# Moving the output projection, two score visits and the masks inside a hand-scheduled attention block

## The chip, the cores and the metric

The kernel runs on one core of one Trainium2 chip. The metric is the device time of one execution in microseconds (us). "Before" is the kernel as it stood, with a median of 557.84 us over three runs.

TensorE (PE in the profile) does matmuls, VectorE (DVE), ScalarE (ACT) and GpSimd (POOL) do the rest, and SyncE (SP) issues the transfers. Each runs its own instruction stream and waits on semaphores.

## The reference, cut to what matters

The input is `x` of 2 sequences of 2048 tokens with 128 features. The reference is one attention layer and one feed-forward layer, each with a normalised residual:

```python
qkv = x @ qkv_w + qkv_b                      # 16 heads of 8
local = softmax(q k^T * scale, dist in (0, 128]) v     # a window of 128 tokens
lattn = softmax(rq rk^T * lscale, over up to 64 pooled latents)
remote = (lattn @ rv) @ rout_w + rout_b
gate = sigmoid(local @ gl_w + remote_h @ gr_w)
mixed = gate * local + (1.0 - gate) * remote_h
y = mixed @ out_w + out_b                    # the output projection
x = x + layernorm(y)
x = x + layernorm(ffn(layernorm(x)))         # 4 experts, argmax router
```

Softmax is computed from a row maximum, so every score is needed twice: once with queries on the partitions (for the maximum) and once with keys on the partitions (for the product with the values).

## The kernel before

**Stages.** The function before `attend` loads, normalises and multiplies by the weights (roughly the first 70 us). `attend` computes both attentions and adds the layer's output to `X`. `ffn` follows; its engines start only when `attend`'s last instructions are done.

**Blocks and steps.** `attend` takes the 4096 tokens as 32 blocks of 128 (`NB` = 32, 16 for each sequence). It runs steps s = -2 to 34, and each engine has one function `emit(s)` with the work of step s in a fixed order. A step works on several blocks at once: the maxima of block s+2, the scores of block s, the latents' product and the values' last part of block s-1, the mixing and projection of block s-2, the output's normalisation of block s-3.

**Visits.** On PE and ACT a step has eight visits g = 0 to 7, each for a pair of heads in both halves. At a visit PE issues:
- `score(s + 2, g, a)` into `psS[g % 2]` (lines 925 to 928), which waits until DVE has taken the maxima of two visits earlier;
- `score_t(s, g, a)` into `psST[g % 2]` (line 961), which waits for the exponentials of two visits earlier;
- then what else belongs to the visit.

**The rest of a step on PE, before the change.** Visit 0: transposes of the latents' probabilities `lprob` of block s-1 (line 1014). Visit 1: `values(s - 1, 3)`. Visit 2: the latents' product into `psC` for block s-1 (line 1025) and the latents' scores (line 1031). Visit 3: transpose of the negated maxima (line 1038), `values(s, 0)`. Visit 4: transposes of `mixed` (line 1049) and of the products with the values (line 1055). Visit 5: `values(s, 1)`. Visit 6: the output projection of block s-2 (line 1064) into `psC`. Visit 7: `values(s, 2)`. These other matmuls are fp32, the scores are bf16.

**Masks.** Scores outside the window must not count. For the visits in `SELECTED` GpSimd sets the exponentials to zero afterwards (`select`, lines 1216 and 1219: two instructions, each 128 x 256). For the other visits PE adds the mask to the bank before the scores (`mask_t`, line 949). The first block of a sequence has all its masks by PE. `values(n, G)` waits for the exponentials of visits 2G and 2G+1 and for the last of the selects that belong to them.

**GpSimd's order in a step before.** The three small operations on the maxima of block s+1 (lines 1230 to 1236); three small operations for the normalisation of block s-3 (`yve`, `yrstd`, `ybias`, lines 1244 to 1249); select of visit 0; `gdiff` and `mixed` of block s-2; selects of visits 2, 3 and 4; `diff` of block s-1 (line 1276); `lprob` of block s (line 1283); select of visit 6; the addition into `X` of block s-3 (line 1290). `select(n, g)` waits for the exponential of visit g.

**ScalarE's order.** At each visit the exponential of that visit (line 1304), and behind it: visit 0 the copy of `lprobT`; visit 2 the copy of the products; visit 3 `mT`; visit 4 `mixedT` and two latent heads' exponentials (line 1343); visit 5 two more; visit 6 `yn` (line 1355); visit 7 `ez`, which waits for `diff`.

**VectorE's order.** Two maxima a visit (line 1084), with others between them: visit 0 `bn_aggr` of block s-3, `ez1`, `gate`; visit 3 the remote part (line 1153) and `lmin`; visit 4 `rden`; visit 5 the local part (line 1180); visit 6 `lrs`; visit 7 `y` (line 1195) and `bn_stats` (line 1199) of block s-2. In the last steps DVE also does, at visit 1, the next stage's `norm.apply` (steps 33 and 34) and `norm.statistics` (steps 32 and 33), and GpSimd does `norm.deviations` near the start of steps 33 and 34.

**Latents.** A block in the first half of its sequence uses 32 latents, one in the second half 64. So `lprob` has 128 or 256 columns, and visits 0 and 2 have one or two rounds.

Of the kernel before, what the change touches and what calls it, by code (L numbers as in the profile page):

```python
# [22 lines left out]
ALU = mybir.AluOpType  # L23
# [3 lines left out]
B, S, D = 2, 2048, 128  # L27
# [27 lines left out]
VW = HZ + 1  # L55
HALF_LAT = NLAT // 2
UN = H // 2
SELECTED = (0, 2, 3, 4, 6)
PAIR_OF_ONES = 1.0 + 2.0 ** -9 - 2.0 ** -16
EPS = 1e-5  # L60
LN_EPS = 1e-12
# [682 lines left out]
def attend(nc, held, for_ffn, norm, ident, identb, filler, eps_col, mhalf, X, lat_k, lat_v, scratch, s_load, s_out):  # L744
    with ExitStack() as ctx:
# [15 lines left out]
        wout, bout, brout, minus1 = held.wout, held.bout, held.brout, held.minus1  # L761
# [25 lines left out]
        mixedT = sb("mixedT", [P, P])  # L787
        y = sb("y", [P, 2, D])
        ystats = sb("ystats", [P, 6])
        ymv = sb("ymv", [P, 2, 2])  # L790
        yve = sb("yve", [P, 1])
        yrstd = sb("yrstd", [P, 1])
        ybias = sb("ybias", [P, 1])
# [7 lines left out]
        psC = ps("psC", [P, 512])  # L801
# [25 lines left out]
        s_local = signal("s_local", "dve")  # L827
# [85 lines left out]
        def _(pe):  # L913
# [75 lines left out]
            def emit(s):  # L989
                for g in range(UN):  # L990
# [9 lines left out]
                    for a in range(2):  # L1000
                        if (s + 2).live:
                            score(s + 2, g, a)
                            if not s.live:
                                beside((psA, psC)[(g + 1) % 2], (g + 1) % 2, 2 * P)
                        if s.live:
                            if not (s + 2).live:
                                beside(psS[g % 2][:].rearrange("p a k -> p (a k)"), g % 2, 2 * P)
                            score_t(s, g, a)
                    if g == 0 and (s - 1).live:
                        n = s - 1  # L1010
                        pe.wait_ge(s_lprob.sem, s_lprob.after(n))
                        pe.wait_ge(s_mixTc.sem, s_mixTc.after(n - 2))
                        for f in range(lat_of(n) // HALF_LAT):
                            last = nc.tensor.transpose(psLP[:, f * P:(f + 1) * P],
                                                       lprob[:, f * P:(f + 1) * P], ident[:])
                        last.then_inc(s_lpT.sem, 1)
# [40 lines left out]
                        last.then_inc(s_pvT.sem, 1)  # L1057
                    if g == 5 and s.live:
                        values(s, 1)
                    if g == 6 and (s - 2).live:  # L1060
                        n = s - 2
                        pe.wait_ge(s_mixTc.sem, s_mixTc.after(n))
                        pe.wait_ge(s_local.sem, s_local.after(n + 1))
                        nc.tensor.matmul(psC[:, 0:D], mixedT[:], wout[:], start=True,
                                         stop=True).then_inc(s_proj.sem, 1)
                    if g == 7 and s.live:
                        values(s, 2)

# [4 lines left out]
        def _(dve):  # L1073
# [48 lines left out]
            def emit(s):  # L1122
                for g, a in ((g, a) for g in range(UN) for a in range(2)):
# [8 lines left out]
                    if (g, a) == (1, 0) and isinstance(s.i, int) and NB <= s.k < NB + 2:  # L1132
                        dve.wait_ge(s_x1.sem, s_x1.after(step(0, CT * (s.k - NB + 1) - 1)))
                        norm.statistics(dve, chunk(s.k - NB))
                    if (g, a) == (0, 0) and (s - 3).live:
                        n = s - 3
                        dve.wait_ge(s_ystats.sem, s_ystats.after(n, 1))
                        stand(dve, s_pass_dve)
                        nc.vector.bn_aggr(ymv[:, n.mod(2)], ystats[:]).then_inc(s_ystats.sem, 1)
# [43 lines left out]
                    if (g, a) == (6, 0) and s.live:  # L1183
# [3 lines left out]
                        if s.mod(RING) == 0:  # L1187
                            dve.wait_ge(s_lrs.sem, s_lrs.after(s))
                            nc.vector.tensor_scalar(lrs[:], lrs[:], valid[:, 1, bass.ds(s.over(RING), 1)],
                                                    None, ALU.mult).then_inc(s_lval, 1)  # L1190
                    if (g, a) == (7, 0) and (s - 2).live:
                        n = s - 2
                        dve.wait_ge(s_proj.sem, s_proj.after(n))
                        dve.wait_ge(s_yn.sem, s_yn.after(n - 2))
                        nc.vector.tensor_tensor(y[:, n.mod(2)], psC[:, 0:D], bout[:], ALU.add).then_inc(s_y.sem, 1)
                    if (g, a) == (7, 1) and (s - 2).live:
                        n = s - 2
                        dve.wait_ge(s_y.sem, s_y.after(n))
                        nc.vector.bn_stats(ystats[:], y[:, n.mod(2)]).then_inc(s_ystats.sem, 1)

# [3 lines left out]
        def _(pool):  # L1204
# [17 lines left out]
            def emit(s):  # L1222
# [14 lines left out]
                      .then_inc(s_neg.sem, 1)  # L1237
                if isinstance(s.i, int) and s.k > NB:
                    norm.deviations(pool, chunk(s.k - NB - 1))
                if (s - 3).live:  # L1240
                    n = s - 3
                    pool.wait_ge(s_ystats.sem, s_ystats.after(n))
                    pool.wait_ge(s_yn.sem, s_yn.after(n - 1))
                    nc.gpsimd.tensor_tensor(yve[:], ymv[:, n.mod(2), 1:2], eps_col[:, 0:1],
                                            ALU.add).then_inc(s_yrstd.sem, 1)
                    pool.wait_ge(s_yrstd.sem, s_yrstd.after(n, 1))
                    nc.gpsimd.tensor_tensor(yrstd[:], yve[:], mhalf[:, 0:1], ALU.pow).then_inc(s_yrstd.sem, 1)
                    pool.wait_ge(s_yrstd.sem, s_yrstd.after(n, 2))
                    nc.gpsimd.tensor_scalar(ybias[:], ymv[:, n.mod(2), 0:1], yrstd[:, 0:1], -1.0, ALU.mult,
                                            ALU.mult).then_inc(s_yrstd.sem, 1)  # L1250
                if s.live:
                    select(s, SELECTED[0])
                if (s - 2).live:
# [12 lines left out]
                                            ALU.add).then_inc(s_mix.sem, 1)  # L1266
                if s.live:
                    select(s, SELECTED[1])
                    select(s, SELECTED[2])
                    select(s, SELECTED[3])  # L1270
                if (s - 1).live:
# [560 lines left out]
```

## Time and profile before

| what | value |
|---|---|
| three runs | 556.84, 557.84, 561.45 us |
| profiled execution | 561.67 us |
| its span, first to last instruction | 560.0 us |
| busy share of the span: PE, DVE, ACT, POOL | 92%, 75%, 53%, 58% |
| mean granted TensorE clock, as a share of full speed | 0.959 |
| length of a step in mid-sequence, 64 latents | 8.62 us |
| length of a step in mid-sequence, 32 latents | 8.41 us |
| last instruction of `attend` ends at | 375.2 us |

The length of a step is the distance between the same matmul in neighbouring steps of the timeline. A row of the timeline gives start, duration, engine, line, operation, tiles and shapes; behind it in brackets stands how long the engine had been idle and what released it. A matmul's duration is modelled, its start is recorded, so distances between starts are the safe reading.

### The profile page before, as it was taken

To read this page: it belongs to the slowest core of one execution; us is meant where nothing else is said; L and a number is where in the kernel's file an instruction comes from. 1 tells how busy PE (TensorE), PEld (TensorE's weight loads), DVE (VectorE), ACT (ScalarE), POOL (GpSimd) and SP (SyncE) were. 2 spreads that over 40 slices of the span, in tenths; PEclk is the share of its full clock that TensorE was granted. 3 is DMA by queue.
4 is the path that set the end of the run, shared out by engine and by line. 5 is a ranking of instruction groups with operands and counts; after the bars stand their busy time and mean duration, and the time that the engine had idled before them with its cause. 6 is when DMAs were issued, how large, how long until landed. Compare 5 with 4: busy or idle time off the path is not lost. (4 is left out here: it accounts for less than half of the span.)

```text
span 560.0 us, 16868 instructions
## 1 busy us (share of the span) xinstructions
PE 515.8 (92%) x5405; PEld 326.1 (58%) x5408; DVE 420.8 (75%) x1952; ACT 298.4 (53%) x820; POOL 325.1 (58%) x759
## 2 busy tenths in 40 slices
PE   8999779999999999999999998869999999999991
PEld 4766424555556665555555665435677677677671
DVE  5876486989888888989898887645647767775655
ACT  2545405888888888888888888612222212211210
POOL 4454301788888888688888889960122342333341
PEclk9999855999999999999999999997999999999997
DMA  4466550434112322222322100000000000000001
GB/s 128 132 193 186 158 104 2 100 88 74 35 41 59 81 62 57 48 36 63 62 63 46 21 4 3 3 1 0 1 2 1 20 17 2 19 19 1 20 19 38
DMA packets 49059, 28.11 MB, mean 50 GB/s; under 512 B 6808, under 2 KB 48056, under 8 KB 48976
## 3 DMA queue, kind: packets, MB, share of 16 engines
q1 hardware_dynamic: 47648, 26.73, 19.7%
q8 instruction: 42, 0.69, 0.5%
q10 hardware_dynamic: 1328, 0.36, 0.3%
q14 instruction: 41, 0.34, 0.2%
HBM read 17.90 MB, written 8.91 MB: 48 GB/s over the span
## 5 line engine op out<-in xcount | busy, mean ns | idle before, releaser
L1084 DVE CUSTOM_DVE_ANT_0 added<-psS,maskq 128x256 bf16<-128x256 f32 x512 | 200.7, 414 | 35.5 <-PE psS L925 22.4
L1304 ACT ACTIVATE probs<-psST 128x512 f32<-128x512 f32 x240 | 143.4, 598 | 42.5 <-PE psST L961 40.9
L961 PE MATMUL psST<-qst,kst 50*128 50x128 bf16 x992 | 100.8, 221 | 0.0
L925 PE MATMUL psS<-kst,qst 48*128 48x256 bf16 x448 | 91.3, 286 | 3.6 <-DVE rowmax L1084 1.6
L982 PE MATMUL psPV<-probs,vst 128*10 128x128 f32 x1984 | 79.7, 276 | 12.7 <-POOL probs L1219 8.9
L1748 ACT ACTIVATE hT<-fpsH 128x512 f32<-128x512 f32 x32 | 19.2, 599 | 121.6 <-PE fpsH L1492 121.6
L1216 POOL TENSOR_SCALAR_AFFINE_SELECT probs<-probs 128x256 f32<-128x256 f32 x150 | 62.1, 414 | 4.1 <-ACT probs L1304 3.5
L925 PEld LDWEIGHTS psS<-kst,qst 48*128 48x128 bf16 x448 | 25.1, 95 | 63.2 <-issue 37.2
L1219 POOL TENSOR_SCALAR_AFFINE_SELECT probs<-probs 128x256 f32<-128x256 f32 x150 | 61.6, 411 | 0.0
L982 PEld LDWEIGHTS psPV<-probs,vst 128*10 128x10 f32 x1984 | 43.9, 91 | 28.1 <-issue 17.4
L1489 PE MATMUL fpsH<-xehi,w1hi 128*128 128x512 f32 x128 | 55.7, 435 | 0.0
L961 PEld LDWEIGHTS psST<-qst,kst 50*128 50x128 bf16 x992 | 55.6, 95 | 0.0
L1489 PE MATMUL fpsH<-xelo,w1hi 128*128 128x512 f32 x128 | 50.6, 395 | 0.0
L1489 PE MATMUL fpsH<-xehi,w1lo 128*128 128x512 f32 x128 | 50.5, 395 | 0.0
L1084 DVE DVE_READ_ACCUMULATOR2_ANT rowmax<- 128x1 f32 x512 | 42.2, 82 | 0.0
L949 PE MATMUL psST<-maskk,identb 128*128 128x512 bf16 (+1 forms) x106 | 39.8, 375 | 0.0
L1731 POOL TENSOR_TENSOR y<-y,gamma 128x512 f32<-128x512 f32 x7 | 9.0, 1293 | 51.9 <-DVE y L1676 51.9
L1343 ACT ACTIVATE lexp<-psA,lmin 128x64 f32<-128x64 f32 (+1 forms) x128 | 37.3, 304 | 0.0
L1668 DVE TENSOR_TENSOR xehi<-fpsE,xfThi 128x512 fp32r<-128x512 f32 x32 | 22.0, 688 | 19.7 <-issue 10.0
L1532 PE MATMUL fpsY<-wo,hT 128*128 128x128 f32 x256 | 30.6, 278 | 0.7 <-ACT hT L1748 0.7
L1489 PEld LDWEIGHTS fpsH<-xehi,w1hi 128*128 128x128 f32 x128 | 24.0, 188 | 11.9 <-issue 8.4
L602 POOL TENSOR_TENSOR early<-resid,early 128x512 bf16<-128x512 f32 x16 | 18.4, 1169 | 20.9 <-ACT early L650 20.9
(198 smaller groups left out, 1111.6 us busy)
## 6 DMA issues: line engine op xcount, KB each, us to landing
q_parts<-early SPq DMA_DIRECT2D x8, 384.0 KB, 2.6
k_parts<-early SPq DMA_DIRECT2D x8, 384.0 KB, 2.7
qst<-q_parts SPq DMA_DIRECT2D x32, 96.0 KB
kst<-k_parts SPq DMA_DIRECT2D x32, 96.0 KB
X<-in_L_attn_x_dram SPq DMA_DIRECT2D x8, 256.0 KB, 3.2
qst<-q_parts SPq DMA_DIRECT2D x32, 64.0 KB
kst<-k_parts SPq DMA_DIRECT2D x32, 64.0 KB
out_dram<-res SPq DMA_DIRECT2D x8, 256.0 KB, 2.3
```

The lines of the kernel that those rows point to most:

```text
L925: last = nc.tensor.matmul(bank[:, a], q, kst[rows, slot, ring(n - 1, 2)], start=True, stop=True)
L949: nc.tensor.matmul(psST[g % 2][:].rearrange("p a (s q) -> p a s q", s=2)[:, :, sides[0]:2], identb[:], maskk[:, sides[0]:2].unsqueeze(1).b ...
L961: last = nc.tensor.matmul(bank[:, a, side * P:(side + 1) * P], kst[rows, slot, ring(n - 1 + side)], qst[rows, slot, ring(n)], start=not ma ...
L982: last = nc.tensor.matmul(psPV[32 * t:32 * t + VW, G * P:(G + 1) * P], vst[:, n.k - 1 + side, SLOTS * (t // 2) + 2 * G + a, :], probs[:, u ...
L1084: taken = nc.vector.tensor_tensor_reduce(added[:, 2 * (g % 2) + a], psS[g % 2][:, a], mask, 1.0, NEG * 4, ALU.add, ALU.max, rowmax[:, n.mo ...
L1216: nc.gpsimd.affine_select(out=before, in_=before, compare_op=ALU.is_gt, fill=0.0, base=0, pattern=[[0, 2], [1 - P, P]], channel_multiplier=P)
L1219: nc.gpsimd.affine_select(out=own, in_=own, compare_op=ALU.is_gt, fill=0.0, base=0, pattern=[[0, 2], [1, P]], channel_multiplier=-1).then_ ...
L1304: nc.scalar.activation(probs[:, g ^ 1], psST[g % 2][:].rearrange("p a c -> p (a c)"), ACT.Exp, scale=SCALE).then_inc(s_exp.sem, 1)
L1343: nc.scalar.activation(per_lat(lexp, s)[:, h], per_lat(psA, s)[:, h], ACT.Exp, bias=lmin[:, s.mod(2), h:h + 1], scale=-1.0, accum_out=lsum ...
L1489: nc.tensor.matmul(psH[j % 2][:], w[:, e, tile], x[:, u, e], start=(e == 0 and k == 0), stop=False)
L1532: last = nc.tensor.matmul(psY[:, t * P:(t + 1) * P], hT[:, m.mod(2), j, t * P:(t + 1) * P], wo[:, j], start=(j == 0), stop=(j == IT - 1))
L1668: nc.vector.tensor_tensor(xehi[:, u, e], psE[e % 2][:], xfThi[:, u].bitcast(F32), ALU.mult)
```

## The change

- PE issues the output projection of block s-3 at visit 0, ahead of the `lprob` transposes, in place of block s-2 at visit 6. It gains a wait for `y` of the block before.
- DVE does `y` and `bn_stats` at visit 1 (block s-3) in place of visit 7 (block s-2), and `bn_aggr` at visit 2 in place of visit 0. In `emit` they stand behind `norm.apply` and `norm.statistics` of visit 1.
- Visits masked by GpSimd become 0, 2, 4, 6 and 7; those masked by PE become 1, 3 and 5. Visit 6 then has only its scores, and visit 7 has no mask.
- GpSimd's order becomes: maxima, select 0, `gdiff`, `mixed`, select 2, `yve`/`yrstd`/`ybias`, select 4, select 6, `diff`, `lprob`, select 7, `X`.

```diff
-SELECTED = (0, 2, 3, 4, 6)
+SELECTED = (0, 2, 4, 6, 7)
...
+                    if g == 0 and (s - 3).live:
+                        n = s - 3
+                        pe.wait_ge(s_mixTc.sem, s_mixTc.after(n))
+                        pe.wait_ge(s_local.sem, s_local.after(n + 1))
+                        pe.wait_ge(s_y.sem, s_y.after(n - 1))
+                        nc.tensor.matmul(psC[:, 0:D], mixedT[:], wout[:], start=True,
+                                         stop=True).then_inc(s_proj.sem, 1)
                     if g == 0 and (s - 1).live:
...
-                    if g == 6 and (s - 2).live:
-                        n = s - 2
-                        pe.wait_ge(s_mixTc.sem, s_mixTc.after(n))
-                        pe.wait_ge(s_local.sem, s_local.after(n + 1))
-                        nc.tensor.matmul(psC[:, 0:D], mixedT[:], wout[:], start=True,
-                                         stop=True).then_inc(s_proj.sem, 1)
...
-                    if (g, a) == (0, 0) and (s - 3).live:
+                    if (g, a) == (2, 0) and (s - 3).live:
                         n = s - 3
                         dve.wait_ge(s_ystats.sem, s_ystats.after(n, 1))
...
-                    if (g, a) == (7, 0) and (s - 2).live:
-                        n = s - 2
+                    if (g, a) == (1, 0) and (s - 3).live:
+                        n = s - 3
                         dve.wait_ge(s_proj.sem, s_proj.after(n))
...
-                    if (g, a) == (7, 1) and (s - 2).live:
-                        n = s - 2
+                    if (g, a) == (1, 1) and (s - 3).live:
+                        n = s - 3
                         dve.wait_ge(s_y.sem, s_y.after(n))
...
                 if s.live:
                     select(s, SELECTED[1])
+                if (s - 3).live:
+                    n = s - 3
+                    pool.wait_ge(s_ystats.sem, s_ystats.after(n))
+                    pool.wait_ge(s_yn.sem, s_yn.after(n - 1))
...
+                if s.live:
                     select(s, SELECTED[2])
                     select(s, SELECTED[3])
                 if (s - 1).live:
```

The added lines in GpSimd's order are those of `yve`, `yrstd` and `ybias`, which leave their place ahead of the first select. The last part of the order stays in place in the code: `diff`, `lprob`, `select(s, SELECTED[4])`, `X`.

## Rows read from the trace of the kernel before

**Rows 1.** Windows, one step with 64 and one with 32 latents; busy us, clock.

```profile
core 0: us, PE busy (x) PEld busy (x) DVE busy (x) ACT busy (x) POOL busy (x), PEclk, DMA share, GB/s
203.04:211.67 8.63, 8.43 (x147) 5.30 (x146) 7.50 (x45) 7.36 (x24) 7.54 (x21) 1.00 0.39 87
245.51:253.92 8.41, 7.91 (x130) 4.92 (x130) 7.43 (x45) 7.16 (x24) 7.33 (x21) 1.00 0.09 25
```

**Rows 2.** Timeline of PE, visits 5, 6, 7 of step 14, then 0.

```profile
209.56 0.23 PE L927 MATMUL psS<-kst,qst 48*128 48x128 bf16 x1
...
210.14 0.62 PE L982 MATMUL psPV<-probs,vst 128*10 128x128 f32 x16 [0.18 <-POOL probs L1219]
210.70 0.23 PE L927 MATMUL psS<-kst,qst 48*128 48x128 bf16 x1
...
210.88 0.22 PE L961 MATMUL psST<-qst,kst 50*128 50x128 bf16 x1
211.03 0.49 PE L1064 MATMUL psC<-wout,mixedT 128*128 128x128 f32 x2
211.36 0.38 PE L949 MATMUL psST<-maskk,identb 128*128 128x512 bf16 x1
211.67 0.23 PE L927 MATMUL psS<-kst,qst 48*128 48x128 bf16 x1
...
212.56 0.28 PE L925 MATMUL psS<-kst,qst 48*128 48x256 bf16 x1
...
212.88 0.44 PE L1014 MATMUL psB<-ident,lprob 128*128 128x128 f32 x2
```

**Rows 3.** Timeline of GpSimd over the same stretch.

```profile
210.89 0.49 POOL L1276 TENSOR_TENSOR diff<-both 128x144 f32<-128x144 f32 x1 [0.17 <-DVE both L1180]
211.89 0.61 POOL L1283 TENSOR_TENSOR lprob<-lexp,lrs 128x256 f32<-128x256 f32 x1 [0.51 <-DVE lrs L1186]
212.45 0.41 POOL L1216 TENSOR_SCALAR_AFFINE_SELECT probs<-probs 128x256 f32<-128x256 f32 x1
212.81 0.41 POOL L1219 TENSOR_SCALAR_AFFINE_SELECT probs<-probs 128x256 f32<-128x256 f32 x1
```

**Rows 4.** Timeline of ScalarE, the exponentials of visits 5 and 6.

```profile
210.04 0.60 ACT L1304 ACTIVATE probs<-psST 128x512 f32<-128x512 f32 x1
...
211.17 0.60 ACT L1304 ACTIVATE probs<-psST 128x512 f32<-128x512 f32 x1
```

**Rows 5.** Timeline of VectorE: the maxima of visit 5, later y.

```profile
210.15 0.42 DVE L1084 CUSTOM_DVE_ANT_0 added<-psS,maskq 128x256 bf16<-128x256 f32 x1 [0.21 <-PE psS L928]
...
210.72 0.41 DVE L1084 CUSTOM_DVE_ANT_0 added<-psS,maskq 128x256 bf16<-128x256 f32 x1
...
212.61 0.29 DVE L1195 TENSOR_TENSOR y<-psC,bout 128x128 f32<-128x128 f32 x1
```

**Rows 6.** Timeline of PE, a step with 32 latents: visits 3, 6, 0.

```profile
250.02 0.62 PE L982 MATMUL psPV<-probs,vst 128*10 128x128 f32 x16 [0.30 <-POOL probs L1219]
...
252.95 0.28 PE L925 MATMUL psS<-kst,qst 48*128 48x256 bf16 x1
...
255.13 0.33 PE L1014 MATMUL psB<-ident,lprob 128*128 128x128 f32 x1
```

**Rows 7.** Timeline of GpSimd in the same step.

```profile
254.13 0.40 POOL L1283 TENSOR_TENSOR lprob<-lexp,lrs 128x128 f32<-128x128 f32 x1 [0.50 <-DVE lrs L1186]
```

**Rows 8.** Timeline of VectorE, the next stage's work in the last steps.

```profile
362.30 0.81 DVE L195 BATCH_NORM_STATS2 stats<-X 128x6 f32<-128x128 f32 x4
...
367.83 1.12 DVE L213 TENSOR_SCALAR xf<-X,mv,rstd 128x128 f32<-128x128 f32 x4 [0.34 <-POOL rstd L207]
```

**Rows 9.** Timeline of GpSimd, the last instruction of `attend`.

```profile
374.73 0.45 POOL L1290 TENSOR_TENSOR X<-X,yn 128x128 f32<-128x128 f32 x1 [0.61 <-ACT yn L1355]
```

**Rows 10.** Windows in the loading stage, around the clock's fall.

```profile
60.00:66.00 6.00, 5.01 (x29) 2.83 (x28) 3.08 (x8) 3.60 (x5) 2.27 (x2) 1.00 0.60 200
66.00:72.00 6.00, 3.15 (x29) 1.74 (x28) 2.99 (x13) 0.00 (x0) 0.00 (x0) 0.58 0.26 71
```

More of the change, by code:

```diff
@@ L1239, in emit @@
                     norm.deviations(pool, chunk(s.k - NB - 1))
[L1240 to L1250, printed above, removed]
                 if s.live:
@@ L1268, in emit @@
                     select(s, SELECTED[1])
+                if (s - 3).live:
+                    n = s - 3
+                    pool.wait_ge(s_ystats.sem, s_ystats.after(n))
+                    pool.wait_ge(s_yn.sem, s_yn.after(n - 1))
+                    nc.gpsimd.tensor_tensor(yve[:], ymv[:, n.mod(2), 1:2], eps_col[:, 0:1],
+                                            ALU.add).then_inc(s_yrstd.sem, 1)
+                    pool.wait_ge(s_yrstd.sem, s_yrstd.after(n, 1))
+                    nc.gpsimd.tensor_tensor(yrstd[:], yve[:], mhalf[:, 0:1], ALU.pow).then_inc(s_yrstd.sem, 1)
+                    pool.wait_ge(s_yrstd.sem, s_yrstd.after(n, 2))
+                    nc.gpsimd.tensor_scalar(ybias[:], ymv[:, n.mod(2), 0:1], yrstd[:, 0:1], -1.0, ALU.mult,
+                                            ALU.mult).then_inc(s_yrstd.sem, 1)
+                if s.live:
                     select(s, SELECTED[2])
```

## The prediction, before the changed kernel was run

> **What bounds the kernel now.** I read the windows first, then the timeline of one step engine by engine. The windows show that in a step of `attend` PE is busy for 8.43 of 8.63 us with 64 latents and 7.91 of 8.41 with 32, while DVE, ACT and POOL each have 7.2 to 7.5 us of work [rows 1]. So PE paces a step, and the others have only about 1 us to spare: a wait of more than that anywhere on the loop becomes the new pace.
>
> The timeline of PE gives the lengths I count with; I write S5 for the start of visit 5, and so on [rows 2]. S5 to S6 is 1.14 us, with a stop before `values` of 0.18 behind POOL's select. A visit with `values` and no stop is 0.89 (S7 to S0). S6 to S7 is 0.97: scores, projection (0.33 from start to start), mask (0.31). At visit 0 the transposes of `lprob` start 0.32 after the scores.
>
> **What decides: the order of GpSimd.** The transposes of `lprob` at visit 0 wait for POOL. Now `lprob` ends at 212.50 and its transposes start at 212.88 [rows 2, 3]: 0.38 us of slack. Now it waits for nothing of visit 6; the select of visit 6 stands behind it. After the change select 6 stands ahead of `diff` and `lprob`, and select 6 must wait for the exponential of visit 6. `diff` and `lprob` are queued behind that wait, and PE's whole stream is queued behind `lprob`. I count from S6:
> - exponential 6 starts. PE alone would allow 0.47 (211.17 against 210.70) [rows 2, 4]. But ACT has other work between exponentials 5 and 6 and takes 1.13 between their starts [rows 4]; with S5 to S6 at only 0.89 that makes 0.47 + 1.13 - 0.89 = 0.71. I take 0.70;
> - its duration 0.60 [rows 4], and 0.05 until POOL starts (estimate, from the 0.05 to 0.1 that starts lie behind ends in these rows);
> - select 6: two instructions 0.36 apart [rows 3], 0.72;
> - `diff` 0.49, of which the next start hides some: 0.45; `lprob` 0.61 [rows 3]; 0.10 until PE starts.
>
> The sum is 3.23 us after S6. Before, it was 212.88 - 210.70 = 2.18. So visit 1 of the next step comes **1.05 us later** after S6. What PE saves between visits 6 and 7 lies inside this wait and is worth nothing. With 32 latents `lprob` takes 0.40 [rows 7]: 3.02 against 255.13 - 252.95 = 2.18 [rows 6], **0.84 us later**. If exponential 6 starts at 0.47 after all, both are 0.23 smaller.
>
> In the Trainium skill, "TensorE: Matmul & The Clock Gate", section "Architectural detail: the array is 16× 32×32, not 1× 128×128", GpSimd's queue is strictly first in, first out. By that rule `diff` and `lprob` can't pass the waiting select, and the sum is the one above; if they could pass, the term of 1.05 would be zero and the result that of the second rival. No row here shows POOL with a ready instruction behind a blocked one; all rows are in program order.
>
> **The other terms of a step.**
> - The mask comes to visit 3, and visit 7's goes away inside the wait. Eight score matmuls, in two streams, start within 0.18 us [rows 2], so 128 columns take about 0.06 and the mask's 512 about 0.22; from above the row at visit 6 gives 0.31. I take +0.22.
> - The latents' product at visit 2 writes `psC` and waits for `y`, which DVE now does at visit 1. DVE starts a visit's first maximum 0.59 after the visit (210.15 against 209.56) [rows 2, 5]; maximum 0.35, `y` 0.29 [rows 5], 0.06 to PE: 1.29 after S1. PE wants it at 0.89 + 0.32 = 1.21. +0.07; between 0 and 0.15.
> - `values(s, 1)` waited for select 3 and now waits for select 2, earlier in POOL's order: S5 to S6 falls from 1.14 to 0.89, -0.25.
> - With 32 latents `values(s, 0)` waits 0.30 for select 0 [rows 6]. Select 0 moves ahead of `yve`, `yrstd`, `ybias`, and visit 3 gets later by the mask: -0.30.
> - The projection in visit 0 (+0.33 less the 0.06 that a first weight load costs anyway) runs while `lprob` is late: 0, if POOL is late as above. Without that cover it is +0.27.
> - DVE, ACT and POOL do the same work as before. `y`, `bn_stats` and `bn_aggr` move to where DVE waits for PE: 0. No transfer moves.
>
> Per step with 64 latents: 1.05 + 0.22 + 0.07 - 0.25 = **+1.09 us**; with 32: 0.84 + 0.22 + 0.07 - 0.25 - 0.30 = **+0.58 us**. Steps 8 to 15 and 24 to 31 are 16 of the first kind. Steps 1 to 7 and 17 to 23 are the second kind; step 1 has little work behind it, so 13. Steps 0 and 16 have no select and are left at zero. 16 x 1.09 + 13 x 0.58 = 17.4 + 7.5 = 24.9 us.
>
> **The end of `attend`.** In steps 32 to 34 there are no scores and the chain is latency. `y` now stands behind the next stage's work in DVE's queue: behind `norm.statistics` (0.81 us of `bn_stats` alone) in step 32, behind `norm.apply` (1.12) and statistics in step 33, behind `norm.apply` in step 34 [rows 8]. What waits for `y` is the latents' product of step 32; then `X` of block 30, which GpSimd adds before the deviations that the second `norm.apply` needs; then the last `X`, now at 374.73 [rows 9], behind which `ffn` starts. None of these was ahead of `y` before. Their sum is 0.81 + 1.12 + 0.81 + 1.12 = 3.9 us; the aggregates behind each statistics and the signals between engines add about 0.9 (estimate, by two stretches of the order of the 0.34 idle and small operations seen there). **+4.8 us**, between 3 (part of it in the idle time ahead of `X`, 0.61) and 6.
>
> The sum is 24.9 + 4.8 = 29.7 us. Against the profiled execution (span 560.0, time 561.67) that is a span of 589.7. The median of the runs shown is 557.84, 3.8 below the profiled execution's time; I put the sum on the median: **587.5 us**.
>
> **Rivals.**
> 1. *As forecast*: POOL's wait for exponential 6 delays `lprob`. 587.5 us.
> 2. *`lprob` is not late, but visit 7 is.* This is what is left if `diff` and `lprob` weren't held up. Visit 7's scores need the maxima of visit 5. The second ends at 211.13, 1.57 after S5 [rows 2, 5], so with 0.07 for the signal S7 is at least S5 + 1.64, where PE alone would allow 0.89 + 0.24 = 1.13. S5 to S7 falls from 2.11 only to 1.64: -0.47. With +0.27, +0.22, +0.07 a step with 64 latents gets 0.09 us longer, and one with 32, after the -0.30, 0.21 shorter. 16 x 0.09 - 13 x 0.21 + 4.8 = +3.5: 561 us. Against it: `lprob` would have to be less than 0.38 us later, and I get 1.05.
> 3. *Faster: PE's saving is realised.* Fewer changes between bf16 and fp32: S6 to S7 falls from 0.97 to 0.24 (-0.73), and +0.27 + 0.22 - 0.25 = -0.49 a step with 64, -0.79 with 32. 16 x 0.49 + 13 x 0.79 = 18.1 us; with no loss at the end 540 us. It decides only if exponential 6 ends so early that select 6, `diff` and `lprob` fit before the transposes and DVE finishes visit 5 within 1.13 us of S5; 0.70 + 0.60 alone is against the first, and the 1.57 read against the second.
> 4. *The clock falls.* PE would stop for about 1 us in every step. The clock was granted at 1.00 through 60 to 66 us, where PE was busy 5.01 of 6, and fell to the lower level of 1.2 GHz in the next stretch, busy 3.15 of 6 [rows 10]. After the change PE would be busy 8.4 of 9.7, above the first of these. If it fell in a quarter of the steps, PE's 8.4 us would double there: 7 x 7 = about 50 us more, 637 us. In the Trainium skill, the same page, section "A second HAM failure mode: psum-queue depth-cycling", short idle gaps between groups of matmuls let the clock swing between its two levels. That rule speaks for this rival; the row of 60 to 66 us speaks against it.
>
> **How the numbers follow.** The forecast 0.80, rival 2 0.07, rival 3 0.05, rival 4 0.03, something else slower 0.05. Low end: exponential 6 at 0.47, no wait for `y`, the end at 3: 16 x 0.79 + 13 x 0.28 + 3 = 19 us, 577; I go to 573 for steps that start late for other reasons, since those absorb part. High end: mask 0.31, `y` 0.15: 16 x 1.26 + 13 x 0.75 + 6 = 36 us, 594, and some 5 more if the clock, idle longer before `ffn`, is low when its matmuls start: 599. The range is 573 to 599. A run of this kernel can tell about 1%, some 5.6 us, from no change. Slower by over 1%: 0.87 (forecast, clock, others). Within 1%: 0.08 (rival 2, and 0.01 of the others). Faster: 0.05.
>
> **What would show it.** Right: POOL idle ahead of the first select instruction of visit 6, released by ACT; PE idle ahead of line 1014, released by POOL `lprob`; steps of about 9.7 us with 64 latents and 9.0 with 32; line 982 hardly waiting for POOL in visits 3 and 5; the last `X` about 30 us later. Wrong: PE waiting for DVE's maxima at visit 7 with no wait at line 1014 would be rival 2; steps shorter than 8.2 us rival 3; granted clock under 1.00 in mid-`attend` rival 4. The least certain is how much of ACT's work lies ahead of exponential 6.

## The result, and the profile after

| | before | after |
|---|---|---|
| median (range) | 557.58 us (556.84 to 561.45) | 592.54 us (590.05 to 595.62) |
| runs | 4 | 4 |
| span of the profiled execution | 560.0 us | 588.3 us |
| mean granted TensorE clock of it | 0.959 | 0.950 |

After is 1.0558 of before, with a 95% interval of 1.0508 to 1.0608. The two medians differ by 35.0 us; 1.0558 of the median before is only 31 us more. The kernel before had medians of 559.6 to 562.34 us in the later series below, and the changed kernel came out 29.6 us above it in its second run, so the loss is best taken as 30 to 35 us. The forecast was 587.5 us, with a range of 573 to 599.

The windows of a step with 64 and one with 32 latents, as in [rows 1] (the two stretches, then busy us and instructions of each engine, granted clock, DMA share and rate):

```profile
core 0: us, PE busy (x) PEld busy (x) DVE busy (x) ACT busy (x) POOL busy (x), PEclk, DMA share, GB/s
195.72:205.38 9.66, 8.38 (x135) 5.26 (x131) 7.77 (x43) 7.39 (x23) 7.54 (x21) 1.00 0.46 88
243.00:251.84 8.84, 7.96 (x119) 4.48 (x118) 8.38 (x49) 7.13 (x25) 5.96 (x17) 1.00 0.05 13
```

Steps take 9.66 us where they took 8.63, and 8.84 where they took 8.41. PE's busy time has hardly changed: the same work, with a stop in it. The timelines of the first step show the stop. GpSimd first, then ScalarE's exponential of visit 6:

```profile
197.14 0.41 POOL L1217 TENSOR_SCALAR_AFFINE_SELECT probs<-probs 128x256 f32<-128x256 f32 x1 [1.64 <-ACT probs L1306]
197.50 0.41 POOL L1220 TENSOR_SCALAR_AFFINE_SELECT probs<-probs 128x256 f32<-128x256 f32 x1
197.88 0.49 POOL L1278 TENSOR_TENSOR diff<-both 128x144 f32<-128x144 f32 x1
198.32 0.61 POOL L1285 TENSOR_TENSOR lprob<-lexp,lrs 128x256 f32<-128x256 f32 x1
```

```profile
196.38 0.60 ACT L1306 ACTIVATE probs<-psST 128x512 f32<-128x512 f32 x1
```

The results that `diff` and `lprob` need from VectorE were there before the select began:

```profile
195.77 0.30 DVE L1181 TENSOR_TENSOR both<-psC,rden 128x144 f32<-128x144 f32 x1
...
196.68 0.17 DVE L1187 RECIPROCAL lrs<-lsum 128x4 f32<-128x4 f32 x1
```

And PE: scores of visit 6, 7 and 0, the projection (L1014), the `lprob` transposes (L1021), the scores of visit 1:

```profile
195.72 0.28 PE L925 MATMUL psS<-kst,qst 48*128 48x256 bf16 x1
...
196.47 0.28 PE L925 MATMUL psS<-kst,qst 48*128 48x256 bf16 x1 [0.35 <-DVE rowmax L1085]
...
197.36 0.28 PE L925 MATMUL psS<-kst,qst 48*128 48x256 bf16 x1
...
197.68 0.49 PE L1014 MATMUL psC<-wout,mixedT 128*128 128x128 f32 x2
198.99 0.44 PE L1021 MATMUL psB<-ident,lprob 128*128 128x128 f32 x2 [0.82 <-POOL lprob L1285]
199.57 0.28 PE L925 MATMUL psS<-kst,qst 48*128 48x256 bf16 x1
```

Read them as one chain. POOL sits idle for 1.64 us in front of the first select instruction of visit 6. `diff` and `lprob`, which don't need that exponential, stand behind it. `diff` was ready at 196.07, when `both` ended, over 1 us before the select started, and GpSimd did not start it ahead of the select. So PE reaches L1021 at 198.99, 3.27 us after visit 6 began, where it was 2.18 [rows 2]. PE did save time between visits 6 and 7 (0.75 where it was 0.97), and waited it away at L1021.

The list of waits from 110 to 370 us adds them up (engine, line, what it waited for: us in total, times, longest us):

```profile
POOL probs L1217 <- ACT probs L1306: 41.7, 33, 1.7
...
PEld psB L1021 <- POOL lprob L1285: 21.9, 27, 1.2
...
ACT ez L1352 <- POOL diff L1278: 15.3, 27, 0.8
```

27 steps with a stop at L1021, where before had none in this list. By stretches of the timeline, the 28.3 us of span between the two profiles are as follows. Below, "mid-`attend`" is the second stretch and "the end of `attend`" the third.

| stretch | before | after | difference |
|---|---|---|---|
| start to step 1's first exponential (unchanged code) | 93.0 | 96.4 | +3.4 |
| to the last exponential (step 31) | 267.9 | 288.5 | +20.5 |
| to the end of the last `X` | 14.3 | 20.6 | +6.3 |
| the rest (`ffn`, unchanged code) | 184.8 | 182.9 | -1.9 |

The first and the last row are differences in unchanged code; the last section shows that they go with the granted clock.

### The profile page after: what moved, and what is told of

Its sections match the earlier page's. It is cut to its first block and busy times, and to the rows that moved or that the text cites. A ratio compares the mean times of both kernels' runs of the same rounds, so it can differ in the third digit from the quotient of the medians.

```text
span 588.3 us, 16868 instructions
## 1 busy us (share of the span) xinstructions
PE 520.0 (88%) x5405; PEld 327.2 (56%) x5408; DVE 429.0 (73%) x1952; ACT 299.5 (51%) x820; POOL 322.8 (55%) x759
```

## The experiments

Ratios are to the kernel before, run beside each experiment on the same chip (median 559.6 us for e1, e2, b1 and b2, 562.34 for e3, e4, c1 and c2, 561.12 for d1, c2 again and after_again). A ratio is the safer number where two series are compared.

### e1: lprob ahead of the select of visit 6

```
                     select(s, SELECTED[2])
-                    select(s, SELECTED[3])
...                                              # diff, lprob
                                             ALU.mult).then_inc(s_lprob.sem, 1)
+                    select(s, SELECTED[3])
                     select(s, SELECTED[4])
```

> The changed kernel with one difference in GpSimd's order: diff and lprob stand ahead of the select of visit 6, with the same five selects and the same amount of work on every engine. Theory A (lprob is late because it is queued behind the wait for exponential 6): no idle time ahead of the latents' transposes; visit 7 waits for VectorE (visit 5 to 7 is 1.64 us); a step with 64 latents 8.6 to 8.7 us, one with 32 latents 8.1 us; 554 to 563 us. Theory B (the projection in visit 0 or the mask in visit 3 is what costs): steps stay near 9.66 and 8.84 us, 588 to 593 us. Theory C (the clock): granted clock below 1.00 in mid-attend, whatever the order.

570.37 us (565.78 to 570.77), ratio 1.0188 [1.0121, 1.0254]. One line moved gives back 22 us by the medians and about 21 by the ratios (1.0558 to 1.0188). GpSimd and PE in a step of it with 64 latents:

```profile
189.85 0.61 POOL L1284 TENSOR_TENSOR lprob<-lexp,lrs 128x256 f32<-128x256 f32 x1 [0.28 <-DVE lrs L1187]
190.42 0.41 POOL L1217 TENSOR_SCALAR_AFFINE_SELECT probs<-probs 128x256 f32<-128x256 f32 x1
```

```profile
188.65 0.28 PE L925 MATMUL psS<-kst,qst 48*128 48x256 bf16 x1
...
189.40 0.28 PE L925 MATMUL psS<-kst,qst 48*128 48x256 bf16 x1 [0.35 <-DVE rowmax L1085]
...
190.61 0.49 PE L1014 MATMUL psC<-wout,mixedT 128*128 128x128 f32 x2
190.94 0.38 PE L1021 MATMUL psB<-ident,lprob 128*128 128x128 f32 x2
...
192.05 0.41 PE L982 MATMUL psPV<-probs,vst 128*10 128x128 f32 x8 [0.19 <-POOL probs L1220]
```

The transposes start 0.33 after the projection, with no stop: 2.29 after visit 6. The 0.35 behind DVE's maxima stays, as in the second rival, and a new small stop shows at visit 1, where `values(s - 1, 3)` waits for the select of visit 7, now last. Steps are 8.77 and 8.13 us, and mid-`attend` takes 268.4 us, where before takes 267.9. The steps came close to what I expected, the time 7 us above the expected range; what is missing lies behind mid-`attend`, as shown under b2.

### e2: the mask of visit 6 by PE

`SELECTED = (0, 2, 4, 7)` in the changed kernel; GpSimd has no select of visit 6.

> The changed kernel with visit 6 masked by TensorE in place of GpSimd (four selects: 0, 2, 4, 7), all orders as changed. Theory A: with no select of visit 6 ahead of diff and lprob, GpSimd doesn't wait for exponential 6 and lprob is early. TensorE pays one mask more (0.22 us), but inside the time in which visit 7 waits for VectorE's maxima of visit 5. 552 to 562 us, steps 8.6 to 8.7 and 8.0 to 8.1 us. Theory B: no better than the changed kernel, rather 0.2 us a step longer, 590 to 600 us.

568.68 us (568.25 to 573.07), ratio 1.0208 [1.0141, 1.0275]; steps of 8.89 and 8.35 us, no stop for `lprob`. Nearly the same comes back by another road (24 us by the medians, 20 by the ratios). GpSimd has one select less here, but in e1 it had all its work: what `lprob` is queued behind, and not the amount of POOL's work, is the cause. PE pays the mask, 0.1 to 0.2 us a step against e1. Here too the time is above the expected 562 us.

### b1: the choice of selects alone, in the kernel before

```
-SELECTED = (0, 2, 3, 4, 6)
+SELECTED = (0, 2, 4, 6, 7)
```

> The kernel before with the selected visits alone changed to 0, 2, 4, 6, 7 (masks by TensorE at 1, 3, 5), so that select 6 stands ahead of diff and lprob; projection at visit 6, yrstd at the start of GpSimd's step, as before. Theory A: most of the slowdown is here: exponential 6 starts 0.66 after visit 6, transposes of lprob 3.27 after it, next visit 0.59 later; with 0.88, 1.45 + 0.22, 0.93, 1.33, 0.88 for visits 1 to 5 a step with 64 latents is 9.55 us, one with 32 latents 8.8 us; no loss at the end of attend; 580 to 586 us. Theory B: within 5 us of the kernel before.

598.25 us (594.95 to 599.47), ratio 1.0707 [1.0641, 1.0773]. The single line costs more than the whole change, 12 us above what I expected. Its windows:

```profile
198.80:208.58 9.78, 8.46 (x136) 5.33 (x133) 7.77 (x43) 7.32 (x23) 7.53 (x23) 1.00 0.49 80
251.43:260.94 9.51, 7.89 (x132) 4.90 (x129) 8.51 (x47) 7.15 (x22) 7.32 (x22) 1.00 0.46 90
```

PE at visit 3 of a step with 32 latents, and GpSimd ahead of it:

```profile
259.13 0.28 PE L925 MATMUL psS<-kst,qst 48*128 48x256 bf16 x1
...
260.38 0.63 PE L982 MATMUL psPV<-probs,vst 128*10 128x128 f32 x16 [0.69 <-POOL probs L1219]
```

```profile
258.39 0.19 POOL L1244 TENSOR_TENSOR yve<-ymv,eps_col 128x1 f32<-128x1 f32 x1
...
259.52 0.41 POOL L1216 TENSOR_SCALAR_AFFINE_SELECT probs<-probs 128x256 f32<-128x256 f32 x1
259.88 0.41 POOL L1219 TENSOR_SCALAR_AFFINE_SELECT probs<-probs 128x256 f32<-128x256 f32 x1
```

POOL comes late out of its wait for exponential 6 and pushes everything behind it: `lprob`, the selects of visit 7, the next step's maxima and statistics, and so the select of visit 0, for which `values(s, 0)` now stops 0.69 us. The whole change moves the statistics behind the select of visit 2, which takes this second stop away: visit 3 of a step with 32 latents is 1.80 us in b1 and 0.93 in the changed kernel. That is why the change costs less than this one line.

I had expected no loss at the end of `attend` here, since `y` and the next stage's work stand as before. It takes 18.5 us, where before has 14.3.

### b2: everything but the choice of selects

`SELECTED = (0, 2, 3, 4, 6)` in the changed kernel.

> The changed kernel with the selected visits as before (0, 2, 3, 4, 6), so the projection at visit 0, y at visit 1 and yrstd behind select 2 are the change alone (GpSimd's order: select 0, mixed, select 2, yrstd, select 3, select 4, diff, lprob, select 6). Theory A: lprob waits for nothing of visit 6. Visit 5 to 7 is 1.7 us (behind VectorE), visit 0 +0.27, y +0.15: a step with 64 latents 8.6 to 8.8 us, one with 32 latents 8.1 to 8.3 us; plus 3 to 5 us at the end of attend: 555 to 564 us. Theory B: 575 us or more.

567.6 us (566.49 to 569.88), ratio 1.0159 [1.0109, 1.0209]; steps of 8.61 and 8.40 us, as before. Moving the projection gains nothing in a step and still costs 1.6%, 4 us more than the top of the expected range. The three kernels without the late `lprob` (e1, e2, b2) are all 8 to 11 us above before with mid-`attend` within 2 us of it, and all have an end of `attend` of 19.3 to 19.6 us where before has 14.3. The next two runs take that end apart.

### e3 and e4: the next stage's normalisation behind y

```
-                    if (g, a) == (1, 0) and isinstance(s.i, int) and s.k > NB:
+                    if (g, a) == (7, 0) and isinstance(s.i, int) and s.k > NB:
                         norm.apply(dve, chunk(s.k - NB - 1))
-                    if (g, a) == (1, 0) and isinstance(s.i, int) and NB <= s.k < NB + 2:
+                    if (g, a) == (7, 0) and isinstance(s.i, int) and NB <= s.k < NB + 2:
```

e3 is the changed kernel with this, e4 is e1 with this.

> The changed kernel with one edit: in steps 32 to 34 VectorE does norm.apply and norm.statistics at visit 7, behind y, bn_stats and bn_aggr, and not at visit 1 ahead of y. Nothing in mid-attend is touched. Theory A for the end of attend (y queued behind the next stage's work): the stretch from the last exponential to the last X falls from 20.6 us to about 15 (before it was 14.3), the projection's result is taken up within 0.5 us of visit 1 in steps 33 and 34, and the time is about 4 to 5 us below the changed kernel: 587 to 589 us. Rival: the longer end is the chain projection, y, bn_stats, bn_aggr, yve of one more visit round, whatever VectorE does beside it; then the end stays over 19 us and the time stays at 592.

> The changed kernel with diff and lprob ahead of the select of visit 6, and norm.apply and norm.statistics behind y as in the run e3. If the two losses add (theory: 22 us from lprob behind exponential 6, 5 from the end), 592.5 - 22.2 - 5 = 565 us; steps of 8.8 and 8.1 us as in e1, the end of attend about 15 us. Rival: the end is not shortened and the time is that of e1, 570 us.

e3: 588.6 us (585.32 to 592.66), ratio 1.05 [1.0419, 1.0581]; the end of `attend` 17.0 us against 20.6, where I had expected about 15. e4: 562.91 us (558.06 to 565.9), ratio 1.002 [0.9982, 1.0058]; the end 14.2 us against e1's 19.3. By its time e3 can't be told from the changed kernel, as the intervals overlap; e4 and e1 are clear of each other. DVE in the last steps of the changed kernel:

```profile
395.04 0.86 DVE L195 BATCH_NORM_STATS2 stats<-X 128x6 f32<-128x128 f32 x4
396.61 0.26 DVE L1196 TENSOR_TENSOR y<-psC,bout 128x128 f32<-128x128 f32 x1
...
401.15 1.11 DVE L213 TENSOR_SCALAR xf<-X,mv,rstd 128x128 f32<-128x128 f32 x4 [3.62 <-POOL rstd L207]
402.18 0.28 DVE L1196 TENSOR_TENSOR y<-psC,bout 128x128 f32<-128x128 f32 x1
```

`y` starts when `norm.apply` lets it go. That `apply` itself had waited 3.62 us for `rstd`, which waits for an earlier `X`, which waits for an earlier `y`: work that the last block needs stood behind a wait of the next stage. With both losses undone, e4 is the kernel before again in time: the two causes together are what the change cost, to within about 0.6% by the interval. (Its steps differ: 8.77 us where before has 8.63, and 8.13 where before has 8.41.)

e3 shows more. Its steps are those of the changed kernel (9.67 and 8.84 us), but mid-`attend` took 291.9 us against 288.5. Its windows around that place, and the changed kernel's at about the same place:

```profile
340.00:345.00 5.00, 4.36 (x79) 2.76 (x70) 4.53 (x25) 5.00 (x18) 2.53 (x8) 1.00 0.02 5
345.00:350.00 5.00, 4.00 (x35) 2.28 (x35) 2.79 (x15) 2.30 (x6) 4.51 (x13) 0.57 0.02 5
350.00:355.00 5.00, 4.97 (x59) 3.07 (x62) 2.69 (x17) 3.01 (x12) 2.25 (x7) 0.75 0.00 1
```

```profile
345.00:350.00 5.00, 3.88 (x46) 2.50 (x46) 3.76 (x21) 3.49 (x8) 4.75 (x14) 1.00 0.01 2
```

In e3 the granted clock fell to its lower level, 1.2 GHz, in mid-`attend`, after PE had been 4.36 of 5 us busy at 2.4 GHz. In the profiled execution of the changed kernel it did not, though PE was no busier (3.88 of 5).

### c1 and c2: the statistics later in GpSimd's order, in the kernel before

`yve`, `yrstd` and `ybias` leave their place ahead of the select of visit 0 (1.13 us of POOL from the first to the select behind it). In c1 they stand behind the select of visit 2, as in the change; in c2 behind the select of visit 4:

```
                     select(s, SELECTED[1])
                     select(s, SELECTED[2])
                     select(s, SELECTED[3])
+                if (s - 3).live:
+                    ...                         # yve, yrstd, ybias
                 if (s - 1).live:
```

> The kernel before with one part of the change alone: yve, yrstd and ybias move behind the select of visit 2 in GpSimd's order. The select of visit 0 then starts up to 1.13 us earlier, as soon as exponential 0 is done. Theory: values(s, 0) waits at visit 3 for that select, 0.22 us in a step with 64 latents and 0.30 with 32 (the wait that my sum missed in steps with 64 latents). It goes: steps of 8.4 and 8.1 us, 16 x 0.22 + 13 x 0.30 = 7.4 us less, about 550 us. The selects of visits 3 and 4 keep their places in time, so the wait at visit 5 stays. Rival: visit 3 doesn't wait with 64 latents, or the time comes back as a longer wait at visit 5 (select 3 is fixed by the work ahead of it, 16 x 0.22 then moves there): 554 to 558 us.

> The kernel before with yve, yrstd and ybias between the select of visit 4 and diff. Now selects 0, 2, 3 and 4 all start up to 1.13 us earlier, and diff is where it was (it waits 0.17 us for VectorE before). Theory: the wait at visit 3 (0.22 or 0.30 us) and the one at visit 5 (0.18 us and more) both go: steps of 8.2 and 7.9 us, 16 x 0.4 + 13 x 0.5 = 13 us less, about 545 us. Rival 1: yve, yrstd and ybias end too late, diff and yn (at ScalarE's visit 6) get late, and ScalarE's later exponentials hold PE: no gain or a loss, 556 us or more. Rival 2: VectorE (7.5 us of work a step) holds PE at visits 6 and 7, and about half is gained, 551 us.

c1: 560.45 us (557.79 to 563.25), ratio 0.9984 [0.9946, 1.0023]; steps of 8.63 and 8.42. The rival was right. PE in a step of c1, visits 3, 4 and 5:

```profile
201.78 0.28 PE L925 MATMUL psS<-kst,qst 48*128 48x256 bf16 x1
...
202.12 0.66 PE L982 MATMUL psPV<-probs,vst 128*10 128x128 f32 x16
202.70 0.28 PE L925 MATMUL psS<-kst,qst 48*128 48x256 bf16 x1
...
204.03 0.28 PE L925 MATMUL psS<-kst,qst 48*128 48x256 bf16 x1
...
204.75 0.62 PE L982 MATMUL psPV<-probs,vst 128*10 128x128 f32 x16 [0.32 <-POOL probs L1219]
```

Visit 3 fell from 1.15 to 0.92 us, and visits 4 and 5 grew from 1.24 to 1.33 and from 1.14 to 1.28: the wait for the select of visit 0 became one for that of visit 3.

c2: 554.06 us (550.18 to 556.74), ratio 0.9866 [0.9806, 0.9926]. Steps are 8.4 and 8.13 us; I expected 8.2 and 7.9 and 545 us, and got the second rival: both stops behind selects are gone (0.22 and 0.26 us with 64 latents), and half of it is lost again at visits 4 (+0.09) and 6 (0.97 to 1.11). Visit 6 began at 211.15 in this step; its projection waits for the local part on VectorE, which PE has now caught up with. PE, then VectorE, then c2's windows:

```profile
211.65 0.46 PE L1064 MATMUL psC<-wout,mixedT 128*128 128x128 f32 x2
```

```profile
211.20 0.30 DVE L1180 TENSOR_TENSOR both<-psC,rden 128x144 f32<-128x144 f32 x1
```

```profile
203.85:212.26 8.41, 8.28 (x147) 5.21 (x146) 7.41 (x44) 7.35 (x23) 7.47 (x22) 1.00 0.52 88
251.48:259.61 8.13, 7.88 (x129) 4.89 (x129) 7.67 (x45) 7.05 (x23) 7.28 (x22) 1.00 0.55 105
```

### d1: what the projection's move is worth with nothing in its way

The change's projection, `y` and statistics, with the masks of before, c2's place of the statistics, and the normalisation behind `y`.

> The changed kernel with the masks of before (GpSimd masks visits 0, 2, 3, 4, 6), with yve, yrstd and ybias behind the select of visit 4, and with norm.apply and norm.statistics behind y in steps 32 to 34. It differs from the run c2 only by the projection, y, bn_stats and bn_aggr of the change (visits 0, 1 and 2 of the next step), and nothing of GpSimd's stands in the projection's way. It measures what the move of the projection is worth by itself. Theory: S5 to S7 falls from the 1.99 us of c2 to the 1.64 that VectorE's maxima allow, visit 0 grows from 0.91 to 1.19 as in the run b2, visit 2 from 1.45 to 1.57 (y), so a step with 64 latents takes 1.64 + 0.89 + 1.19 + 0.88 + 1.57 + 0.93 + 1.33 = 8.43 us against 8.38: the saving is given back, 554 to 557 us. Rival (PE's saving is realised once POOL is out of the way): steps under 8.2 us, 548 us.

> The kernel of the run c2 once more (before, with yve, yrstd and ybias between the select of visit 4 and diff), so that d1 has its neighbour on the same chip. 0.980 to 0.993 of the kernel before, as its first run had it; steps of 8.4 and 8.1 us.

d1: 554.4 us (550.9 to 555.46), ratio 0.9897 [0.9851, 0.9944]. c2 again: 555.92 us (550.05 to 557.09), ratio 0.9901 [0.9859, 0.9942]. They can't be told apart; both beat both kernels, by 1% to 1.3% over before. d1's windows:

```profile
190.39:198.80 8.41, 8.27 (x139) 5.23 (x133) 7.55 (x43) 7.26 (x23) 7.54 (x23) 1.00 0.13 35
251.25:259.22 7.97, 7.80 (x129) 4.94 (x129) 7.49 (x43) 6.95 (x23) 7.26 (x22) 1.00 0.34 56
```

With 64 latents the step is c2's: from visit 5 to 7 it saves 0.36 us, and visits 0 and 2 pay 0.28 and 0.12. With 32 it is 0.16 shorter, 2 us in 13 steps, below what the runs can tell. The saving is real and is given back in the same step.

### after_again: the changed kernel once more

> The changed kernel once more. In the run e3, whose steps before the end are the same as the changed kernel's, the granted clock fell in mid-attend at 345 to 353 us and at 225 to 230 us, and some executions of the changed kernel have a mean clock of 0.936 where its profiled one has 0.95. If longer stops of PE in a step make such a fall a matter of chance, this kernel's executions spread in mean clock between 0.935 and 0.95 and by 5 us in time, and the profiled one may show a fall between 110 and 370 us; the median is 590 to 595 us and the steps are 9.66 and 8.84 us where the clock is full. Rival: the clock is at 1.00 in all of mid-attend, and the fall in e3 belongs to its edit.

590.68 us (587.8 to 597.61), ratio 1.0532 [1.0462, 1.0603]. Its four executions had mean clocks of 0.950, 0.950, 0.941 and 0.935 at 587.8, 588.6, 592.8 and 597.6 us; the four of its first run, 0.950 at 590.1 us and 0.941 to 0.936 at 591.0 to 595.6. The profile is that of the longest, and shows a fall in mid-`attend` at 165 to 175 us:

```profile
160.00:165.00 5.00, 4.61 (x73) 2.89 (x74) 4.42 (x25) 4.37 (x16) 3.85 (x11) 1.00 0.41 59
165.00:170.00 5.00, 4.25 (x57) 2.26 (x55) 3.51 (x20) 2.92 (x7) 4.33 (x13) 0.74 0.01 2
170.00:175.00 5.00, 5.00 (x44) 3.31 (x45) 2.44 (x14) 1.91 (x5) 2.50 (x7) 0.58 0.02 3
```

and two more at 225 to 235 and 345 to 355. So the same code falls in one execution and not in another. Between 110 and 350 us only this profile and e3's show a fall. Full clock there have all the profiles without the stop at `lprob` (before, e1, e2, b2, e4, c1, both of c2, d1), but also the first profile of the changed kernel and b1, whose steps are the longest. And e4, without the stop, falls a little later, still ahead of its last exponential at 365.2 us:

```profile
355.00:360.00 5.00, 3.54 (x36) 2.41 (x35) 3.46 (x9) 2.05 (x4) 4.92 (x10) 0.79 0.00 0
```

So the stop is neither needed for a fall nor enough for one. That it makes falls in mid-`attend` more likely is possible (two of four profiles with it, none of nine without, up to 350 us) and not shown.

## Why the prediction was right, point by point

**The main term, lprob behind the wait for exponential 6.** Right in place and size. Against its sum, piece by piece: exponential 6 at +0.66 (forecast 0.70), 0.60 long, POOL's start 0.16 behind its end (forecast 0.05), select 6 0.74, `diff` 0.44, `lprob` and the signal 0.67. The transposes came at 3.27 for 3.23. Undone in two ways (e1, e2) it returned 22 to 24 us by the medians, 20 to 21 by the ratios. The prediction said that no row showed POOL with a ready instruction behind a blocked one; `diff`, ready at 196.07 and started at 197.88 behind the select, is such a row. By distances between score starts, visit 6 to visit 1 grew by 1.09 us with 64 latents and by 0.83 with 32; the forecast was 1.05 and 0.84.

**Mask at visit 3 and y at visit 2.** Together 0.29, measured 0.33 in both kinds of step (visit 2 with 64 latents grew from 1.45 to 1.78). In b2, which has `y` there but no mask at visit 3, it is 1.57: so `y` costs 0.12, where I had 0.07 (1.29 less 1.21 is 0.08; I had written 0.07), and the mask 0.21, where I had 0.22. b1, with the mask and no `y`, has 1.66: the same 0.21. DVE's `ez1` had also got late (it waits 0.26 for `ez`, which waits 0.55 for `diff`), and `y` is queued behind that.

**Visit 5.** -0.25 forecast, -0.26 measured.

**The projection in visit 0.** The 0.06 of a first weight load was not in the rows shown. What it served for was the price without cover, +0.27; b2, e1 and d1 show visit 0 grown by 0.26 to 0.27.

**Visit 3, the step that was mis-sized.** I counted the wait for the select of visit 0 as zero with 64 latents and 0.30 with 32, because the bracket of the `values` row says so: none, and 0.30 [rows 6]. Measured by the distance from visit 3 to visit 4, it was 0.22 (1.15 fell to 0.93) and 0.48 (1.41 to 0.93). The bracket counts from PE's last modelled end, and at visit 3 the transpose of the maxima covers part of the wait. I had said myself that starts are the safe reading, and then took the bracket. Visit 4 grew by 0.09, which I didn't have: the transposes of `mixed` (L1056) wait for the copy `mT`, which starts 0.96 to 0.98 us after visit 3 in both kernels, however early PE gets to visit 4; c1 shows the same 0.09 with no mask involved. With 32 latents visit 1 also fell by 0.08 (0.97 to 0.89). Steps then grew by 1.04 and 0.43 us where I had 1.09 and 0.58: 16 x 1.04 + 13 x 0.43 = 22.2 us, and 20.5 measured from step 1 to the last exponential, where I had 24.9. Steps at a change of sequence or of latents absorb the rest.

**The end of attend.** Forecast +4.8 (3 to 6), measured +6.3. The mechanism is shown by e3 and e4 (-3.6 and -5.1 us of it). What I left out: `norm.apply` took 1.45 us there beside other work where its row before had 1.12 [rows 8], and PE, mostly waiting in this stretch, ran at the lower clock for two stretches (next section). With e3's edit alone 2.7 us of the 6.3 stay; with `lprob` in time as well (e4) the end is 14.2 us, before's 14.3. b1 says the same from the other side: with the late `lprob` and `y` as before, the end is 4.3 us longer. So the new order of the selects lengthens the end by itself, which my sum didn't have. In these stretches the clock was at its lower level for 6.8 us in e3 and 10.2 in b1, and not at all in before and e4; how much is the clock and how much the wait was not taken apart.

**The sum.** 24.9 + 4.8 was to be 29.7 us; the spans differ by 28.3, the medians by 35.0. Of the spans' difference +3.4 lie in the loading stage, which the change doesn't touch (below). The medians differ by more than the spans because the profiled execution of after is its fastest and that of before its slowest; my putting the sum on the median of before, 3.8 us under its profiled execution, was the weaker of two choices. That 28.3 lies so near 29.7 is partly luck: the steps cost 4.4 us less than forecast and the end 1.5 more, and the loading stage and `ffn`, which were not in the sum, gave +3.4 and -1.9.

**The rivals.** The second (visit 7 late behind DVE's maxima) is there as a mechanism: S5 to S7 is 1.63 us where I had 1.64. It is hidden behind L1021 in the changed kernel, and sets the pace in e1 and d1. The third (PE's saving) is settled by d1: 0.36 us are saved and 0.40 paid. The fourth, the clock in mid-`attend`, got 0.03 and should have been part of the forecast in a small size: not a quarter of the steps, but up to three falls in an execution. In e3 the windows at 225 to 230 and 345 to 355 us show clocks of 0.66, 0.57 and 0.75, which is about 10 us at the lower level. By the trace's clock, mid-`attend` of e3 has 8.8 us more at the lower level than that of the changed kernel (which begins with more left of the loading stage's low clock) and takes 3.5 us more; that of `after_again` has 14.9 more and takes 6.1 more. That is 0.4 us for each, not the doubling that I took for a step. The likely reason, not tested, is that a step is also paced by waits for the other engines.

In the Trainium skill, "TensorE: Matmul & The Clock Gate", section "A second HAM failure mode: psum-queue depth-cycling", short idle gaps of PE between groups of matmuls let the clock swing. The falls in e3 and `after_again` agree with that; the profiled execution of the changed kernel and b1, with the same or longer gaps and full clock from 110 to 350 us, don't show it, and e4 fell without the gap at `lprob`. No run here shows that the gaps decide.

## What to carry to other kernels

An engine that executes in order makes everything behind a wait late, so before moving an instruction forward, ask when its input is ready and who reads the results queued behind it: one changed line of `SELECTED` cost 7% here, mainly because it put the wait for exponential 6 ahead of `lprob`. Work of the next stage, too, belongs behind the last work of this one, not ahead of it. And read a wait as the distance between two recorded starts against the same distance without the wait; the bracket of idle time showed 0 here where the distance was 0.22 us, and 0.30 where it was 0.48.

## What the runs showed of the hardware

- **GpSimd starts later behind ScalarE than I took.** Exponential 6 ends at 196.98 and the select starts at 197.14: 0.16 us. The other stops of this kind in the changed kernel and in b1 have 0.16 to 0.17.
- **GpSimd did not pass a waiting instruction with a ready one.** `diff` had all its inputs at 196.07 and started at 197.88, behind the select that waited for exponential 6. With the order changed (e1) it did not wait.
- **The clock differs between executions of the same code.** The loading stage is unchanged. Before kept the full clock through 46 to 58 us; in the profiled execution of after it fell there, and step 1's first exponential came 3.4 us later:

```profile
46.00:52.00 6.00, 6.00 (x31) 4.20 (x30) 3.99 (x15) 1.09 (x2) 1.92 (x3) 0.68 0.74 207
52.00:58.00 6.00, 6.00 (x32) 3.93 (x30) 1.50 (x2) 3.08 (x6) 2.26 (x2) 0.75 0.49 161
```

  Of the thirteen profiles of all runs, four keep the full clock there and reach that exponential at 92.1 to 93.0 us; nine fall and reach it at 95.0 to 96.4. The executions of c1 also lie in two groups, 557.8 to 559.3 us at a mean clock of 0.958 to 0.959 and 561.6 to 563.3 at 0.953; only one of them, of the second group, was profiled, and it fell there. A difference of 4 us between two single profiles of this kernel means nothing.
- **The clock also falls around the end of `attend`, and `ffn` pays for what is left of it.** At the end of `attend` the changed kernel has

```profile
390.00:395.00 5.00, 4.04 (x12) 1.94 (x12) 2.33 (x8) 0.72 (x2) 3.11 (x7) 0.50 0.01 3
...
405.00:410.00 5.00, 3.17 (x12) 2.23 (x12) 0.00 (x0) 1.23 (x2) 1.69 (x2) 0.50 0.00 0
```

  two separate falls where before has one; the second reaches into the first microseconds of `ffn`. The code behind `attend` is the same in all runs: it took 181.5 us in e3, with full clock, 184.7 to 184.8 in before and c1, with 6.8 us of it at the lower level, and 185.8 in e2, with 10.4 us of it. A longer end needs no low clock, though: in e1 it is 19.3 us and the clock falls only in its last 0.5 us. That longer waits cause the falls was not tested.
